# First and last rounds of an attention layer reordered; weight means in one matmul each, table load and tensor engine started early

## The reference, cut to what matters

```python
B, T, D, H, Dh, E, R = 32, 256, 128, 16, 64, 8, 16
x = x + ln(attn(ln(x)))        # Q, K, V = ln(x) @ W + b; softmax(Q K^T / 8) V; @ W_O + b_O
x = x + ln(ffn(ln(x)))
def ffn(x):                    # per token
    gate = softmax(x @ gate_w.T)
    t = einsum('nh,erh->ner', x, lora_U)
    return x @ weight.T + einsum('ne,eor,ner->no', gate, lora_V, t) / R
```

## Time and profile before

| | us |
|---|---|
| median of 3 runs (lowest, highest) | 1220.92 (1219.39, 1223.68) |
| the profiled execution | 1221.85 |
| span in the profile | 1220.0 |

### The profile page before, as it was taken

The page is one execution under the profiler, slowest core; times in us unless marked ns, Lnnn a source line. Parts: engine busy times, 40 slices in busy tenths (PEclk is TensorE's granted clock), DMA queues, the critical chain, the costliest instruction groups (busy, mean ns, idle before and its releaser), DMA issues.

```text
span 1220.0 us, 32981 instructions
## 1 busy us (share of the span) xinstructions
PE 1185.9 (97%) x10532; PEld 977.1 (80%) x10532; DVE 958.6 (79%) x2618; ACT 967.9 (79%) x3079; POOL 728.3 (60%) x946
## 2 busy tenths in 40 slices
PE   6899999999999999999999999999999999999995
PEld 3688888888888888888888888888888888888883
DVE  4677888887888887887877878877888878788883
ACT  2678888888888888888888888888888888888882
POOL 2556556665556665566665666675556665555653
PEclk9899999999999999999999999999999999999997
DMA  6000000000000000000000000000000000000000
GB/s 213 2 1 6 2 6 4 4 4 4 0 4 4 4 4 4 0 4 4 4 4 4 4 0 4 4 4 4 4 0 4 4 4 4 4 0 4 4 4 9
DMA packets 9923, 10.95 MB, mean 9 GB/s; under 512 B 816, under 2 KB 9392, under 8 KB 9904
## 3 DMA queue, kind: packets, MB, share of 16 engines
q1 hardware_dynamic: 9904, 10.70, 2.7%
HBM read 6.50 MB, written 4.19 MB: 9 GB/s over the span
## 4 chain that ended last, share of the span: by engine, by line
PE 82%; POOL 7%; DVE 6%; issue 4%; ACT 1%; POOLq 0%; DVEq 0%; DMA 0%; SPq 0%; ACTq 0%
PE o_ps L383 17%; PE st_ps L365 17%; PE st_ps L355 14%; PE extra_ps L398 8%; PE qk_ps L304 4%; PE qk_ps L306 4%; PE qk_ps L305 4%; POOL probs L1021 3%; PE extra_ps L337 3%; PE extra_ps L339 2%; PE extra_ps L338 2%; DVE probs_t L806 2%; PE extra_ps L270 2%; POOL xn L1010 1%; POOL xn L1015 1%
## 5 line engine op out<-in xcount | busy, mean ns | idle before, releaser
L1021 POOL TENSOR_TENSOR probs<-probs,inv_sum 128x512 f32<-128x512 f32 x512 | 525.4, 1042 | 352.6 <-DVE inv_sum L801 342.0
L563 ACT ACTIVATE probs<-st_ps,neg_max 128x256 f32<-128x256 f32 x1024 | 475.2, 482 | 102.6 <-DVE neg_max L794 99.7
L794 DVE TENSOR_REDUCE neg_max<-st_ps 128x2 f32<-128x512 f32 x512 | 332.0, 680 | 48.8 <-PE st_ps L355 45.7
L365 PE MATMUL st_ps<-ident,probs 128*128 128x128 f32 x2048 | 286.6, 275 | 6.7 <-POOL probs L1021 5.1
L365 PEld LDWEIGHTS st_ps<-ident,probs 128*128 128x128 f32 x2048 | 233.9, 141 | 46.9 <-POOL probs L1021 21.6
L383 PE MATMUL o_ps<-probs_t,v_sb 128*64 128x256 f32 x2048 | 256.3, 387 | 0.3 <-DVE o_lo L812 0.2
L563 ACT ACTIVATION_READ_ACCUMULATOR probs<-st_ps,neg_max 128x1 f32 x1024 | 217.1, 212 | 0.0
L806 DVE COPY probs_t<-st_ps 128x512 f32<-128x512 f32 x256 | 169.4, 683 | 37.4 <-PE st_ps L365 37.3
L383 PEld LDWEIGHTS o_ps<-probs_t,v_sb 128*64 128x64 f32 x2048 | 133.4, 136 | 73.2 <-issue 5.9
L778 DVE TENSOR_TENSOR qk_lo<-qk_ps,qk_hi 128x512 fp32r<-128x512 f32 x256 | 175.1, 684 | 11.8 <-ACT qk_hi L550 11.5
L571 ACT COPY probs_t<-st_ps 128x512 f32<-128x512 f32 x256 | 152.5, 596 | 32.6 <-PE st_ps L365 32.6
(11 more groups left out here) (116 smaller groups left out, 2073.4 us busy)
## 6 DMA issues: line engine op xcount, KB each, us to landing
out<-x_all SPq DMA_DIRECT2D x32, 128.0 KB, 1.7
x_all<-in_x SPq DMA_DIRECT2D x1, 3840.0 KB, 17.3
stage_v<-in_w_v SPq DMA_DIRECT2D x1, 512.0 KB, 4.1
stage_o<-in_w_o SPq DMA_DIRECT2D x1, 512.0 KB, 6.7
stage_q<-in_w_q SPq DMA_DIRECT2D x1, 384.0 KB, 4.7
stage_k<-in_w_k SPq DMA_DIRECT2D x1, 384.0 KB, 5.8
x_all<-in_x SPq DMA_DIRECT2D x2, 128.0 KB, 3.1
ffn<-in_ffn_w SPq DMA_DIRECT2D x1, 196.0 KB, 6.8
```

What stands on the lines that cost most here:

```text
L365: last = nc.tensor.transpose(st_ps[p % 2][h][:, s * T + j * P:s * T + (j + 1) * P], probs[p % N_PROBS][h][:, j, s * P:(s + 1) * P], ident[ ...
L563: last = nc.scalar.activation(probs[n][h][:, j, :], st_ps[p % 2][h][:, j * T:(j + 1) * T], ACT.Exp, bias=neg_max[n][h][:, j:j + 1], accum_ ...
L794: nc.vector.tensor_reduce(neg_max[p % N_PROBS][h][:, :], st_ps[p % 2][h][:, :].rearrange("p (j s) -> p j s", j=NT), AX.X, ALU.max, negate= ...
L1021: nc.gpsimd.tensor_tensor(probs[n][h][:, :, :], probs[n][h][:, :, :], inv_sum[n][h][:, :].unsqueeze(2).to_broadcast([P, NT, T]), ALU.mult) ...
```

## The change

Four things are changed. The unrolled bodies 0 to 2 and 32 to 33 are written out step by step on each engine in a new order; the loop's body keeps its order and its waits. Weight means are one matmul for each of 6 pieces: POOL makes the bias diagonal and then subtracts the weight from it (`bias_less_weight`), so the second matmul of each piece is gone. V's weights are no longer centred or given their bias: their column sums (8 float32 matmuls of one column, in `ffn_means`) and the bias go through W_O into the output bias (`centre_ffn_columns`, `output_bias` with 9 matmuls of one column, `centre_output_bias`). ACT begins with a copy of one column as soon as the constants are there, and PE with 12 float32 matmuls of 128 columns on constants (`warm_up`). POOL computes the q and k pieces of pairs 0 and 1 ahead of the first `ln_rstd`, and all others ahead of the first `scale_probs`.

```diff
+WARM_UPS = 12
...
@@ -209,16 +204,14 @@
         MEANS = (
             ("q", slice(0, 256), st_ps[0][0], slice(0, 256)),
             ("k", slice(0, 256), st_ps[0][1], slice(0, 256)),
-            ("v", slice(0, 512), st_ps[1][0], slice(0, 512)),
-            ("v", slice(512, 1024), st_ps[1][1], slice(0, 512)),
             ("q", slice(256, 512), o_ps, slice(0, 256)),
-            ("q", slice(512, 1024), st_ps[0][0], slice(0, 512)),
-            ("k", slice(256, 512), st_ps[1][0], slice(0, 256)),
-            ("k", slice(512, 1024), st_ps[0][1], slice(0, 512)),
+            ("q", slice(512, 1024), st_ps[1][0], slice(0, 512)),
+            ("k", slice(256, 512), o_ps, slice(0, 256)),
+            ("k", slice(512, 1024), st_ps[1][1], slice(0, 512)),
         )


-        diag_home = {"v": 1, "q": 2, "k": 3}
+        diag_home = {"q": 2, "k": 3}

         def diag(n, cols):
             half = probs[diag_home[n]][cols.start // HALF][:, :, :].rearrange("p j s -> p (j s)")
...
+            def warm_up():
+
+                for _ in range(WARM_UPS):
+                    nc.tensor.matmul(st_ps[1][1][:, 0:P], mean_w[:, :], mean_w[:, :], start=True, stop=True)
+
+            def weight_means(piece):
+
+                n, cols, bank, dst = MEANS[piece]
+                if piece == 4:
+                    pe.wait_ge(mean_folded, 3)
+                pe.wait_ge(diag_ready[n], 1 if piece < 2 else 2 if cols.stop <= HALF else 3)
                 nc.tensor.matmul(bank[:, dst], mean_w[:, :], diag(n, cols),
-                                 start=True, stop=False)
-                nc.tensor.matmul(bank[:, dst], neg_mean_w[:, :], stage[n][:, cols],
-                                 start=False, stop=True).then_inc(mean_projected, 1)
-
-            def transpose_xn(b, free):
-                after(pe, *free)
+                                 start=True, stop=True).then_inc(mean_projected, 1)
+
+            def ffn_means():
+
+                pe.wait_ge(mean_folded, 5)
+                pe.wait_ge(ffn_rows_centred, 1)
+                nc.tensor.matmul(o_ps[:, 0:D + TG], mean_w[:, :], ffn[:, F_W:F_W + D + TG],
+                                 start=True, stop=True)
+                pe.wait_ge(w_loaded["v"], 16)
+                for pair in range(PAIRS):
+                    last = nc.tensor.matmul(o_ps[:, D + TG + pair:D + TG + pair + 1],
+                                            stage["v"][:, pair_cols(pair)], one[:, 0:1],
+                                            start=True, stop=True)
+                last.then_inc(ffn_means_projected, 1)
+
+            def output_bias():
+
+                pe.wait_ge(v_offset_ready, 1)
+                pe.wait_ge(ffn_ready, 1)
+                pe.wait_ge(w_o_centred, 1)
+                dst = o_ps[:, D + TG + PAIRS:D + TG + PAIRS + 1]
+                nc.tensor.matmul(dst, neg_mean_w[:, :], bias[:, B_O:B_O + 1], start=True, stop=False)
+                for pair in range(PAIRS):
+                    last = nc.tensor.matmul(dst, stage["o"][:, pair_cols(pair)], v_offset[:, pair:pair + 1],
+                                            start=False, stop=(pair == PAIRS - 1))
+                last.then_inc(bias_o_projected, 1)
...
+            warm_up()
+            weight_means(0)
+            weight_means(1)
+            transpose_xn(0)
+            project_qk(0, 0)
+            project_qk(0, 1)
+            weight_means(2)
+            project_v(0, 0, free=(xt_lo_ready, 1))
+            weight_means(3)
+            weight_means(4)
+            project_v(0, 1, free=(v_copied[0], 1))
+            scores(0, 0)
+            weight_means(5)
+            ffn_means()
+            scores(0, 1)
+            project_v(0, 2, free=(v_copied[1], 1))
+            project_qk(0, 2, free=(qk_lo_ready, 1))
+            project_qk(0, 3, free=(qk_lo_ready, 2))
+            output_bias()
+            transpose_probs(0, 0, 1, free=(exp_ready[1], 1))
+            project_qk(0, 4, free=(qk_lo_ready, 3))
+            project_qk(0, 5, free=(qk_lo_ready, 4))
+            transpose_probs(0, 1, 1, free=(exp_ready[1], 2))
+            transpose_probs(0, 0, 0, free=(exp_ready[0], 1))
+            transpose_probs(0, 1, 0, free=(exp_ready[0], 2))
+            project_v(0, 3, free=(v_copied[2], 1))
+            scores(0, 2, free0=(probs_t_copied[0], 1), free1=(probs_t_copied[1], 1))
+            scores(0, 3, free0=(probs_t_copied[0], 2), free1=(probs_t_copied[1], 2))
...
+            probs_v(31, 2, free=(o_lo_ready, 125))
+            transpose_probs(31, 4, 1, free=(exp_ready[1], 253))
+            transpose_probs(31, 5, 1, free=(exp_ready[1], 254))
+            project_tg(30, free=(x1t_ready, 31))
+            transpose_probs(31, 5, 0, free=(exp_ready[0], 254))
+            scores(31, 6, free0=(probs_t_copied[0], 253), free1=(probs_t_copied[1], 253))
+            probs_v(31, 3)
+            scores(31, 7, free0=(probs_t_copied[0], 254), free1=(probs_t_copied[1], 254))
+            transpose_u(30, free=(u_ready, 31))
+            probs_v(31, 4, free=(o_lo_ready, 126))
+            probs_v(31, 5)
+            transpose_probs(31, 6, 1, free=(exp_ready[1], 255))
+            project_z(30, free=(ut_ready, 31))
+            transpose_probs(31, 6, 0, free=(exp_ready[0], 255))
+            transpose_probs(31, 7, 1, free=(exp_ready[1], 256))
+            output_projection(31, 0, free=(z_copied, 31))
+            transpose_probs(31, 7, 0, free=(exp_ready[0], 256))
+            probs_v(31, 6, free=(o_lo_ready, 127))
+            probs_v(31, 7)
+            output_projection(31, 1)
+            output_projection(31, 2)
+            output_projection(31, 3)
...
+            nc.scalar.copy(seen_one[:, :], one[:, :])
+            weight_hi("q", early, early_hi_ready, 1)
+            weight_hi("k", early, early_hi_ready, 2)
+            xt_high(0)
+            weight_hi("v", every, w_hi_ready)
+            qk_hi(0, 0)
+            qk_hi(0, 1)
+            copy_v(0, 0)
+            weight_hi("q", late, w_hi_ready, 4)
+            copy_v(0, 1)
+            weight_hi("o", every, w_hi_ready)
+            weight_hi("k", late, w_hi_ready, 6)
+            exponentials(0, 0, 0)
+            exponentials(0, 0, 1)
+            qk_hi(0, 2)
+            qk_hi(0, 3)
+            exponentials(0, 1, 1)
...
+                nc.vector.tensor_tensor(v_offset[:, :], bias[:, B_V:B_V + PAIRS],
+                                        o_ps[:, D + TG:D + TG + PAIRS], ALU.subtract
+                                        ).then_inc(v_offset_ready, 1)
                 nc.vector.tensor_tensor(ffn[:, F_W:F_W + D + TG], ffn[:, F_W:F_W + D + TG],
-                                        o_ps[:, 0:D + TG], ALU.subtract)
+                                        o_ps[:, 0:D + TG], ALU.subtract).then_inc(ffn_ready, 1)
+
+            def centre_output_bias():
+                dve.wait_ge(bias_o_projected, 1)
                 nc.vector.tensor_tensor(bias[:, B_O:B_O + 1], bias[:, B_O:B_O + 1],
-                                        o_ps[:, D + TG:D + TG + 1], ALU.subtract).then_inc(ffn_ready, 1)
+                                        o_ps[:, D + TG + PAIRS:D + TG + PAIRS + 1],
+                                        ALU.add).then_inc(bias_o_ready, 1)
...
+            stats_x(0)
+            norm_first_x()
+            fold_means(0)
+            fold_means(1)
+            weight_lo("q", early, early_hi_ready, early_lo_ready)
+            weight_lo("k", early, early_hi_ready, early_lo_ready)
+            xt_low(0)
+            stats_x(1)
+            weight_lo("v", every, w_hi_ready, w_lo_ready)
+            qk_lo(0, 0)
+            fold_means(2)
+            qk_lo(0, 1)
+            w_o_means()
+            fold_means(3)
+            fold_means(4)
+            centre_ffn_rows()
+            weight_lo("q", late, w_hi_ready, w_lo_ready)
+            fold_means(5)
+            row_max(0, 0, 1)
+            row_max(0, 0, 0)
+            centre_ffn_columns()
+            weight_lo("k", late, w_hi_ready, w_lo_ready)
+            row_max(0, 1, 1)
+            invert_sum(0, 0, 1)
+            invert_sum(0, 0, 0)
+            row_max(0, 1, 0)
+            qk_lo(0, 2)
+            qk_lo(0, 3)
+            invert_sum(0, 1, 1)
+            copy_probs_t(0, 0)
...
+            def bias_less_weight(n, column, pair, end):

                 shape = [P, end - pair, P]
+                cols = slice(pair * P, end * P)
+                pool.wait_ge(bias_loaded, 16)
                 nc.gpsimd.tensor_tensor(
-                    diag(n, slice(pair * P, end * P)).rearrange("p (n c) -> p n c", c=P),
+                    diag(n, cols).rearrange("p (n c) -> p n c", c=P),
                     ident[:, :].unsqueeze(1).to_broadcast(shape),
                     bias[:, column + pair:column + end].unsqueeze(2).to_broadcast(shape),
-                    ALU.mult).then_inc(diag_ready[n], 1)
+                    ALU.mult).then_inc(diag_made[n], 1)
```

(115 more changed lines are left out.)

1003 lines of the change are left out of this document (627 added, 376 removed).

## The result

| | before | changed |
|---|---|---|
| median of the runs on the same chip, us | 1221.70 (4 runs, 1219.39 to 1223.68) | 1208.55 (4 runs, 1207.95 to 1209.62) |
| ratio, 95% interval | | 0.9894 [0.9877, 0.9911] |
| span of the profiled execution, us | 1220.0 | 1207.8 |
| first projection on PE | 13.37 | 11.42 |
| projection of pair 2 | 28.82 | 25.05 |

The prediction was 1207.6 us, with a range of 1201.5 to 1213.5. The span is 12.2 us shorter, and the landmarks split it: the head gives 12.7, the tail 1.3, and the 28 rounds from the loop's first step to the last batch take 1.8 back (28 x 0.065). Their means are 12.2 us apart.

A forecast was written before the change was run, and what follows sets the result against it. PE was taken to bound the loop at 36.4 us a round, leaving only the ends to gain: head 11.9 and tail 1.4, so 1220.9 - 13.3 = 1207.6 us, with a range of 1201.5 to 1213.5.

The forecast's parts named there:

- Head, first projection: Kernel start: after x's norm, folds and low parts, first projection on PE at 11.3 us against 13.37.
- Low parts on DVE each lasting over 1 us beside POOL: Sign of a wrong forecast, before the first projection; low parts were counted at 0.35 us each.
- Head, pair 2's projection and scores: Before the loop: pair 2's projection at 24.0 us, not 28.82; its scores at 32.0 against 42.38, 10.4 us gained.
- Head, behind pair 2: From pair 2's scores to the loop: 1.5 us off 86.4, with some 5 us idle or half clock left.
- pairs 2 to 7 of batch 0 have the same chain between them: Reason given for leaving some 5 us of idle or half-clock loss between pair 2's scores and the loop.
- rival (1): Head: later losses go too, up to 4 of 5 us, and POOL hardly stops DVE, 1.6; 1202.0 us, chance 0.15.
- is no term of its own: Head: PE's removed matmul columns mostly stood in waits, so no separate gain was counted for them.
- Tail: Kernel end: output projection's group 0 and z go before the last transposes, saving 1.4 us, bounds 0.5 and 3.
- Rounds in the loop of 36.4 as before: Sign of a right forecast: loop rounds unchanged; a difference over 0.1 us would show it wrong.
- (2): Head held by latency and clock, including two more half-clock stretches (3.2 us): 7.3 us less, 1213.6, chance 0.15.
- (3): Loop entered with POOL late, lag staying 29 rounds; 0.46 us each cancels the gain, 0.6 gives 1225; chance 0.04.
- (4): Head: DVE's list keeps pair 2's projection at 28.8; only tail and 1.5 us remain, 1218 us, chance 0.06.

The follow-up runs named there:

- the repeated profile: The changed kernel run once more with nothing altered, beside later variants: 1208.36 us, ratio 0.9901 to the kernel before.
- the fillers: Changed kernel plus 11 float32 matmuls of 128 columns on PE between the first transpose and the first projection: 1208.37 us, ratio 0.9900.
- both kernels that isolate it: Old kernel with only the last two bodies reordered: 1219.69 us, ratio 0.9995; changed kernel with those bodies in the old order: 1209.04 us, 0.9911.

## Why the prediction was right, and where it wasn't

**Head, first projection: right in this profile, with luck.** 11.42 against 11.3, and the parts held: rstd at 7.5 (7.15), xn's end at 8.4 (8.3), low parts and xt_low at 11.3 (11.2). The low parts met POOL once, which the 11.2 between the two bounds had room for. "Low parts on DVE each lasting over 1 us beside POOL" was named as what would be wrong. One was (1.26), and in the repeated profile both (1.12 and 1.48) with the first projection at 12.33, beyond the bound of 11.6: that bound was too tight, as one stop costs up to 1.1 us (1.48 against 0.41), and there were two. The repeated profile of the changed kernel:

```profile
8.44 0.73 POOL L1400 TENSOR_TENSOR probs<-probs,stage_q 128x256 f32<-128x256 f32 x1 [0.26 <-DMA stage_q<-in_w_q]
```
```profile
9.32 1.12 DVE L950 SCALAR_TENSOR_TENSOR wq_lo<-stage_q,wq_hi 128x256 fp32r<-128x256 f32 x1 [0.15 <-ACT wq_hi L681]
10.37 1.48 DVE L950 SCALAR_TENSOR_TENSOR wk_lo<-stage_k,wk_hi 128x256 fp32r<-128x256 f32 x1
```

What decides is when the rest of W_Q lands and sets POOL off. Where POOL went on at 8.32 to 8.52, both low parts were stopped and the first projection came at 12.21 to 12.41 (three profiles); where it went on at 8.75 to 9.06, one was, and it came at 11.42 to 11.78 (three, one of them with the fillers). The prediction's own landing, 8.3, belongs to the first kind, where these rows give some 12.3 and not 11.3. POOL's subtraction takes 0.72 for 256 columns and 1.28 to 1.33 for 512, not 0.6 and 1.04; that hid behind the rest. Nor are the six diagonals of the earlier trace rows all of 512 columns: by the pieces in `MEANS` they are four of 512 and two of 256, so 0.86 is a mean of two sizes, and the changed kernel's rows have 1.04 and 0.61.

**Head, pair 2's projection and scores: mechanism right, one term missed.** 25.05 against 24.0, and 34.38 against 32.0, 8.0 us gained and not 10.4. The list of work was right: with half clock only from 10.9 to 14.1 and the first projection at 11.32 the same code gave 23.79 and 32.0. What failed is that the sum had no term for half clock between the first projection and pair 2, although it kept the old kernel's loss for later. In the changed kernel the low clock lay in just that part: 10.5 to 17.3 and 24.1 to 27.5. output_bias took its 1.9 us (taken 2.0), at 27.59.

**Head, behind pair 2: mis-sized the other way.** From pair 2's scores to the loop the prediction took 1.5 us off 86.4 and left 5 us of waits and half clock as they were. It was 81.7, so 4.7 off (it is 81.7 in all five profiles of this head, wherever it began). The step that failed is "pairs 2 to 7 of batch 0 have the same chain between them": the chain is there, but PE isn't idle in it, 22.57 busy of 22.60 us at full clock where the earlier trace rows had 2.3 us of waiting and 1.6 of half clock. This is the mechanism of rival (1), which got 0.15; its other half, that POOL hardly stops DVE, is wrong. The two misses of 2.4 and 3.2 us cancel to 0.8 us of head, 12.7 against 11.9. That the total came out right is luck to this extent, and isn't evidence for its parts.

**Removed PE work "is no term of its own": half right.** Its columns were miscounted: two matmuls for each of the eight pieces are 6144 columns, one for each of six 2048, so 4096 went. The account shows 3.1 us less work, and with PE nearly without idle time that became time. But putting the work back for W_Q and W_K (101.9 us of work) didn't lengthen the kernel, as its price came back through POOL, DVE and the clock. So the single matmul is not what made the kernel faster. What did is the rest of the head, by the 7.0 us of idle time that it removes, with the earlier first projection; the early table load is worth about 1.1 us, the warm-ups nothing that can be measured. How the gain divides between the new order and V's weights, whose centring and bias left the path of the first V steps, no run shows: none has the one without the other.

**Tail: right.** 1.3 against 1.4, in both kernels that isolate it, by the step that the prediction named.

**Loop: the one thing held to be unchanged that changed.** "Rounds in the loop of 36.4 as before" held by its bound of 0.1, but 28 x 0.065 = 1.8 us is more than the tail gives. Addresses make 0.046 of it in one pair of kernels and 0.045 in the other, 1.3 us over 28 rounds, though a round differs by up to 0.03 between profiles of one code. Of the last 0.01 to 0.02 a third is one round: the loop's first takes 36.54 to 36.65 us with every new head and 36.35 to 36.37 with the old one. Which of the loop's tensors feels its address wasn't tried.

**Rivals (2) to (4).** Of (2) the clock was real, but inside the normal spread: profiles of new heads start the loop between 113.06 and 117.11 us. Its price was added wrongly: a gain of 13.3 less 7.3 is 6.0 and gives 1214.9 us, not 1213.6, which is 1220.9 less 7.3; so rival (2) at its full price lay outside the range. (3) needed 0.46 us for each round; the rounds lost 0.065, most of it by addresses. (4) is out: pair 2's projection is 3.8 us earlier.

## What to carry to other kernels

Cut the head at landmarks and write it as start, idle time, half clock and work at full clock, for each of two profiles of the same code: it shows at once which term an order moves, and that 3 us of it may be chance. Before moving work from a busy engine to POOL, see whether DVE has two SBUF inputs at that moment; a 0.4 us operation can cost 1.5. Try new small tensors behind those that the loop uses. And look at the spacing of the matmuls before trusting a clock of 1.00 at a kernel's start.

## What was not expected of the hardware

- PE fell to 1.2 GHz at 24.1 us straight after 6.80 of 6.80 busy us at 2.4 GHz (1.8 of them in one-column matmuls), and filling the idle time ahead of the first projection moved the low stretch (to 20.9 to 27.7, in another profile 23.5 to 26.9) and didn't remove it.
- Allocating two tensors of one and eight float32 columns ahead of the loop's tensors, not behind them, changed the mean of a 256-column matmul from 279 to 281 ns and the round by 0.045 us, in two pairs of kernels.
- One execution's head differs from the next by the clock and by when one load lands: the old head ended at 128.80, 127.33 and 126.17, the new one at 117.11, 116.08, 114.81, 114.56 and 113.70.
